# Shared experts of the second layer: fp32 matmuls replaced by three fp32r products of high and low parts

## What is computed

```python
scores = softmax(xt @ gate_w.T); _, idx = top_k(scores + gate_bias, 2)
for e in range(8):
    h = silu(xt @ w1[e].T) * (xt @ w3[e].T)
    y = y + gate_e[:, None] * (h @ w2[e].T)
z = silu(xt @ sw1.T) * (xt @ sw3.T) @ sw2.T        # the shared experts: 512 hidden numbers
return y + z
```

## Time and profile before

| | |
|---|---|
| median of 3 runs | 1104.73 us (1104.25 to 1109.32) |
| the profiled execution | 1107.14 us, of it 1105.3 us from the first to the last instruction |
| granted TensorE clock, mean | 0.894 |
| busy: TensorE, VectorE, GpSimd, ScalarE | 904.4, 696.2, 538.2, 441.5 us |
| gate and up of layer 1's shared experts (L1585) | 128 records, 66.1 us busy |
| their down products (L1632) | 128 records, 28.6 us busy |

### The profile page before, as it was taken

The page is one execution under the profiler, slowest core; times in us unless marked ns, Lnnn a source line. Parts: engine busy times, 40 slices in busy tenths (PEclk is TensorE's granted clock), DMA queues, the critical chain, the costliest instruction groups (busy, mean ns, idle before and its releaser), DMA issues.

```text
span 1105.3 us, 20321 instructions
## 1 busy us (share of the span) xinstructions
PE 904.4 (82%) x5372; PEld 692.5 (63%) x5373; DVE 696.2 (63%) x2004; ACT 441.5 (40%) x1030; POOL 538.2 (49%) x575
## 2 busy tenths in 40 slices
PE   3468888887297999999999904879999996998893
PEld 2357777777144888888888502545656563787672
DVE  6669999996664865555555256765868246443334
ACT  4558888992051444444444302122322313232220
POOL 7246656644004755555552577874700000687641
PEclk9679999995556999999999966969999998899997
DMA  8860000003101777777768738342300011466647
GB/s 248 212 123 3 1 0 0 0 1 107 43 1 51 220 219 202 224 215 220 214 192 138 281 95 278 105 141 80 112 6 20 1 61 23 82 111 127 139 75 243
DMA packets 75225, 127.42 MB, mean 115 GB/s; under 512 B 12481, under 2 KB 52033, under 8 KB 75009
## 3 DMA queue, kind: packets, MB, share of 16 engines
q0 software_dynamic: 21264, 48.02, 19.5%
q1 hardware_dynamic: 32240, 57.47, 17.1%
q10 hardware_dynamic: 21632, 20.85, 5.4%
HBM read 80.62 MB, written 36.77 MB: 106 GB/s over the span
## 4 chain that ended last, share of the span: by engine, by line
PE 60%; DVE 19%; issue 6%; DMA 6%; POOL 3%; ACT 2%; SPq 2%; DVEq 0%; ACTq 0%; POOLq 0%
PE bank L899 18%; PE bank L914 9%; PE bank L1585 5%; PE bank L888 4%; DVE ptl L609 4%; PE bank L801 3%; DMA sw<-in_w 3%; POOL yg L1178 3%; PE bank L1485 3%; DVE nmax L601 2%; PE bank L907 2%; PE bank L419 2%; DVE x L1193 2%; PE bank L1520 2%; PE bank L1632 2%
## 5 line engine op out<-in xcount | busy, mean ns | idle before, releaser
L1163 POOL DMA_INDIRECT xg<-token_rows,gather_idx x198 | 190.7, 963 | 318.3 <-DMA token_rows<-cw 135.6
L899 PE MATMUL bank<-sw,xgt 128*128 x948 | 247.5, 384 | 0.0
L899 PEld LDWEIGHTS bank<-sw,xgt 128*128 128x128 f32 x948 | 167.6, 193 | 15.2
L1178 POOL DMA_INDIRECT yg<-slot_rows,slot_of x128 | 137.0, 1070 | 70.3 <-issue 33.5
L992 ACT ACTIVATE ssil<-bank 128x128 f32<-128x128 f32 x237 | 65.7, 278 | 202.1 <-PE bank L899 202.1
L914 PE MATMUL bank<-sw,sht 128*128 x474 | 145.0, 388 | 0.0
L1084 DVE COPY xgt<-bank 128x256 f32<-128x256 f32 x198 | 83.9, 424 | 85.4 <-PE bank L888 77.3
L1097 DVE COPY sht<-bank 128x128 f32<-128x128 f32 x237 | 69.1, 291 | 106.4 <-PE bank L907 106.1
L537 ACT ACTIVATE prob<-bank,nmax 128x256 f32<-128x256 f32 x256 | 111.7, 511 | 7.5 <-DVE nmax L601 7.5
L419 PE MATMUL bank<-consts,prob 128*128 128x128 f32 x512 | 83.5, 288 | 34.7 <-DVE ptl L609 32.2
L601 DVE TENSOR_REDUCE nmax<-bank 128x2 f32<-128x512 f32 x128 | 87.6, 685 | 16.6 <-PE bank L406 15.7
(11 more groups left out here) (216 smaller groups left out, 1570.5 us busy)
## 6 DMA issues: line engine op xcount, KB each, us to landing
slot_rows<-ysb ACTq DMA_DIRECT2D x79, 256.0 KB, 3.4
sw<-in_w SPq DMA_DIRECT2D x48, 384.0 KB, 3.6
kst<-khl SPq DMA_DIRECT2D x32, 224.0 KB, 5.6
token_sums<-zeros SPq DMA_DIRECT2D x2, 2176.0 KB, 12.1
token_rows<-xn SPq DMA_DIRECT2D x8, 512.0 KB, 3.6
sums<-token_sums SPq DMA_DIRECT2D x8, 512.0 KB, 7.2
xg<-token_rows,gather_idx POOLq DMA_INDIRECT x198, 3.5
x<-in_x SPq DMA_DIRECT2D x4, 512.0 KB, 6.7
```

The source lines that it names most:

```text
L899: mm = pe.matmul(bank[2 + k % 2][:, 0:2 * FF], xgt[:, i % 3, c * P:(c + 1) * P], w[:, :, c, :], start=(c == 0), stop=(c == CH - 1))
L1163: nc.gpsimd.indirect_dma_start(xg[:, (first + i) % XG_RING, 0:ROW[L]], None, rows[L], bass.IndirectOffsetOnAxis(gather_idx[:, i:i + 1], 0) ...
L1178: nc.gpsimd.indirect_dma_start(yg[:, t % Y_TILES, j, :], None, ybuf[L], bass.IndirectOffsetOnAxis(slot_of[:, t, j:j + 1], 0)).then_inc(s_y ...
```

## The change

Both sides of the shared experts' matmuls of layer 1 are split into a high part (the fp32 number copied to the type fp32r) and a low part (the number less its high part, as fp32r), and each fp32 product becomes three fp32r products: high by high, high by low, low by high, summed in PSUM.

- The weights are split once at the start of the stage. They are loaded into two tiles that are used later in the stage (`prob1`, and `hq` as `down_raw`), now ahead of the parameters on SyncE's queue; ScalarE makes `whi` by four copies, VectorE makes `wlo` by four subtractions between its first and its second `y_pair_added`.
- The inputs: after `inputs_copied`, ScalarE makes `xh` (two copies of 512 columns, `inputs_high`), and VectorE makes `xl` (two subtractions, `inputs_low`), placed ahead of `logits_taken`. `shared_gate_up(b, 0)` waits for `xl`.
- The hidden numbers: ScalarE makes `hh` (`hidden_high`, one copy for each of 4 units), and `hl` (`hidden_low`, one subtraction for each) is made by VectorE for batches 0 and 3 and by GpSimd, behind all its gathers, for batches 1 and 2. For batch 3 this happens inside the expert blocks of layer 1. `shared_down` waits for `hl`.

```diff
...
-        wsh1 = sb("wsh1", [P, SH1, WCOLS], F32)
+        whi = sb("whi", [P, SH1, WCOLS], F32R)
+        wlo = sb("wlo", [P, SH1, WCOLS], F32R)
+        xh = sb("xh", [P, CH, SEQ], F32R)
+        xl = sb("xl", [P, CH, SEQ], F32R)
...
+                if L == 1 and 2 <= k < 2 + 2 * SH1 and k % 2 == 0:
+                    hidden_high(act, m, BATCH - 1, (k - 2) // 2)
...
+                if L == 1 and 6 <= k < 6 + 2 * SH1 and k % 2 == 0:
+                    hidden_low(dve, nc.vector, BATCH - 1, (k - 6) // 2)
...
-                if b == 1:
-                    sp.dma_start(wsh1[:, :, :], w1_in[0:SH1].rearrange("u p c -> p u c")).then_inc(m.wload, 16)
...
                 if u == 0:
                     pe.wait_ge(A["p"], 4 * min(b + 2, BATCH))
+                    pe.wait_ge(A["xlo"], CH * (b + 1))
...
-                        mm = pe.matmul(bank[half][:, :], wsh1[:, u, w], xt[:, 0, c, :], start=(c == 0), stop=(c == CH - 1))
+                        for wp, xp in ((whi, xh), (whi, xl), (wlo, xh)):
+                            mm = pe.matmul(bank[half][:, :], wp[:, u, w], xp[:, c, :], start=(n == 0), stop=(n == 5))
+                            n += 1
...
-            pe.wait_ge(m.h, m.n["h"] + SH1 * (b + 1))
+            pe.wait_ge(A["hlo"], SH1 * (b + 1))
...
-                    mm = pe.matmul(bank[6 + j // 2][:, (j % 2) * DIM:(j % 2 + 1) * DIM], hid1[:, u, j * P:(j + 1) * P],
-                                   wsh1[:, u, 2 * CH * FF:WCOLS], start=(u == 0), stop=(u == SH1 - 1))
+                    for hp, wp in ((hh, whi), (hh, wlo), (hl, whi)):
+                        mm = pe.matmul(bank[6 + j // 2][:, (j % 2) * DIM:(j % 2 + 1) * DIM], hp[:, u, j * P:(j + 1) * P],
+                                       wp[:, u, 2 * CH * FF:WCOLS], start=(n == 0), stop=(n == 3 * SH1 - 1))
+                        n += 1
...
+        def hidden_high(act, m, b, u):
+            act.wait_ge(m.h, m.n["h"] + SH1 * b + u + 1)
+            nc.scalar.activation(hh[:, u, :], hid1[:, u, :], ACT.Copy).then_inc(A["hhi"], 1)
+
+        def hidden_low(eng, ops, b, u):
+            eng.wait_ge(A["hhi"], SH1 * b + u + 1)
+            ops.tensor_tensor(hl[:, u, :], hid1[:, u, :], f32(hh[:, u, :]), ALU.subtract).then_inc(A["hlo"], 1)
...
+            def inputs_high(b):
+                if b:
+                    act.wait_ge(m.up, m.n["up"] + SH1 * b)
+                for c in range(CH):
+                    act.wait_ge(m.xh, m.n["xh"] + 2 * b + c + 1)
+                    nc.scalar.activation(xh[:, c, :], xt[:, 0, c, :], ACT.Copy).then_inc(A["xhi"], 1)
...
+            def inputs_low(b):
+                for c in range(CH):
+                    dve.wait_ge(A["xhi"], CH * b + c + 1)
+                    nc.vector.tensor_tensor(xl[:, c, :], xt[:, 0, c, :], f32(xh[:, c, :]), ALU.subtract).then_inc(A["xlo"], 1)
...
             y_pair_added(dve, 0, 0)
+            n = 0
+            for part, source in ((gate_up_cols, prob1), (down_cols, down_raw)):
+                for u in range(0, SH1, 2):
+                    n += 1
+                    dve.wait_ge(A["whi"], n)
+                    nc.vector.tensor_tensor(wlo[:, u:u + 2, part], source[:, u:u + 2, :], f32(whi[:, u:u + 2, part]),
+                                            ALU.subtract).then_inc(A["wlo"], 1)
             y_pair_added(dve, 0, 2)
...
                 encoder(b)
+                if b == 2:
+                    hidden_low(dve, nc.vector, 0, 3)
...
                 if b:
+                    inputs_low(b - 1)
                     logits_taken(b - 1)
...
+                if b == 1:
+                    hidden_low(dve, nc.vector, 0, 0)
                 products(b)
...
         def pool_a1(pool):
             for t in range(TILES):
                 y_gathered(pool, 0, t)
+            for b in (1, 2):
+                for u in range(SH1):
+                    hidden_low(pool, nc.gpsimd, b, u)
...
```

More of the change, by code:

```diff
@@ L134, in gated_xattn_moe_kernel @@
         wsh0 = sb("wsh0", [P, WCOLS], F32)
-        wsh1 = sb("wsh1", [P, SH1, WCOLS], F32)
+        whi = sb("whi", [P, SH1, WCOLS], F32R)
+        wlo = sb("wlo", [P, SH1, WCOLS], F32R)
+        xh = sb("xh", [P, CH, SEQ], F32R)
+        xl = sb("xl", [P, CH, SEQ], F32R)
         hid1 = sb("hid1", [P, SH1, SEQ], F32)
+        hl = sb("hl", [P, SH1, SEQ], F32R)
+        hh = sb("hh", [P, SH1, SEQ], F32R)
         lg1 = sb("lg1", [P, TILES, E1], F32)
@@ L201, in gated_xattn_moe_kernel @@
         hq = sb("hq", [P, CH, SEQ], F32, a1)
+        down_raw = hq[:, :, :].rearrange("p c (a f) -> p (c a) f", f=DIM)
+        gate_up_cols, down_cols = slice(0, 2 * CH * FF), slice(2 * CH * FF, WCOLS)
         prod = sb("prod", [P, CH, SEQ], F32, a1)
@@ L330, in gated_xattn_moe_kernel @@
             "msim", "mx", "mxt", "nmx", "gmx", "ngmx", "eb", "ebr", "hb", "hbc", "w14", "hq", "hqh", "prod", "o", "x",
-            "one", "bg", "bx")}
+            "one", "bg", "bx", "whi", "wlo", "xhi", "xlo", "hhi", "hlo")}
         s_out = sem("out_stored")
@@ L1576, in shared_gate_up @@
                 if v == 0:
-                    pe.wait_ge(m.wload, 16)
+                    pe.wait_ge(A["wlo"], SH1)
                 else:
@@ L1650, in softmax @@
             def softmax(b):
+                if b == 0:
+                    act.wait_ge(A["wlo"], SH1)
                 for j in range(TPB):
@@ L1680, in shared_silu @@
                 nc.scalar.activation(hid1[:, u, :], bank[0][:, :], ACT.Silu).then_inc(m.sil, 1)
+            def inputs_high(b):
[4 more added lines that the diff above has]
+                    nc.scalar.activation(xh[:, c, :], xt[:, 0, c, :], ACT.Copy).then_inc(A["xhi"], 1)
+            act.wait_ge(m.wload, 32)
+            for part, source in ((gate_up_cols, prob1), (down_cols, down_raw)):
+                for u in range(0, SH1, 2):
+                    nc.scalar.activation(whi[:, u:u + 2, part], source[:, u:u + 2, :], ACT.Copy).then_inc(A["whi"], 1)
             for b in range(BATCH):
@@ L1686, in scalar_a1 @@
                     inputs_copied(b - 1)
+                    inputs_high(b - 1)
                     shared_silu(b - 1, 0)
@@ L1692, in scalar_a1 @@
                     for u in range(1, SH1):
+                        hidden_high(act, m, b - 1, u - 1)
                         shared_silu(b - 1, u)
+                    hidden_high(act, m, b - 1, SH1 - 1)
             b = BATCH - 1
             inputs_copied(b)
+            inputs_high(b)
             act.wait_ge(m.rs, 2)
@@ L1849, in vector_a1 @@
                 weights_by_bar(b)
+                if b == 1:
+                    hidden_low(dve, nc.vector, 0, 1)
                 if b:
@@ L1853, in vector_a1 @@
                     y_pair_added(dve, 0, 4 * b + 6)
+                    if b == 1:
+                        hidden_low(dve, nc.vector, 0, 2)
                     stats_of_summed(dve, b + 1)
@@ L1864, in vector_a1 @@
             shared_added(dve, m, b - 1)
+            inputs_low(b)
             logits_taken(b)
@@ L1935, in _ @@
             sp.wait_ge(s_sye, BLOCKS[0])
+            raw = w1_in[0:SH1].rearrange("u p c -> p u c")
+            sp.dma_start(prob1[:, :, :], raw[:, :, 0:2 * CH * FF]).then_inc(moe[1].wload, 16)
+            sp.dma_start(down_raw, raw[:, :, 2 * CH * FF:WCOLS]).then_inc(moe[1].wload, 16)
             parameters_a1(sp)
```

1 line of the change is left out of this document (added).

## The result

The changed kernel took **1124.17 us** (median of 4 runs, 1121.90 to 1126.22) beside 1106.54 us (1104.25 to 1109.32) of the kernel before (4 runs): a ratio of 1.0168, 95% interval 1.0133 to 1.0204. The forecast was 1111, reckoned from the median of 1104.73 of the three runs known then, with a range of 1101 to 1120: the sign was right, the size was not, and the time lies outside the range. The profiled execution took 1126.22 us (span 1124.3, mean clock 0.880) against 1107.14 (1105.3, 0.894).

The account below looks back on a forecast made before the run. TensorE was taken to bound the kernel, VectorE close behind. Turns' shift 0, clock +4.3 and weights' split +2 summed to +6.3 us on the profiled 1107.14; against the median of 1104.73 the forecast was 1111, range 1101 to 1120.

Parts of the forecast that it names:

- TensorE's saving: Shared experts' matmuls: 0.9 us saved per gate and up unit, 1.5 per down product; 20.4 us in all, 18.9 to be won.
- Turn 1: Transposes of turn 2 come 1.7 us earlier; VectorE, making `xn` late, has become the bound there.
- The two waits: Turn 2: TensorE idles 4.4 us before the down product for `hl`, 3.1 behind the logits for `xl`; turn 3 repeats it.
- the clock term: New gaps in turns 2 and 3 bring 2.5 falls to half clock, 1.7 us each: +4.3 us, bounds 0 to 9.
- the forecast gain of 1.9: Batch 3: faster units take back about 1.9 us, so the shift is 0 when the expert blocks begin.
- the split: Stage start: VectorE's four weight subtractions lengthen a GpSimd gather, +2 us, bounds 0 and 3.8; `whi` costs nothing.
- Its literal reading: Port lock held over the back-to-back weight subtractions: split term 3.8 us, sum 1.8 us more; not used in the sum.
- The expert blocks: Layer 1: the four `hh` and `hl` fit between a block's other steps, priced at 0; without cover 4 x 0.65 us.
- (a): Rival: the saving comes through as operands are ready before TensorE asks; about 14 us won, 1091 us; chance 0.14.
- (b): Rival: waits as forecast, but no more clock falls and gathers don't suffer; shift 0, about 1105 us; chance 0.24.
- (c): Rival: half clock through most of turns 2 and 3, or slow fp32r matmuls at 512 columns; 1119 to 1135 us; chance 0.12.

Follow-up runs that it names:

- early_split: Changed kernel with raw weights loaded during layer 0 and split by GpSimd in idle time ahead of its gathers; 1117.82 us, ratio 1.0110.
- reordered: Changed kernel with turns 2 and 3 reordered: down products halved around the scores, input low parts ahead of the shared experts' addition, normalisation later; 1113.68 us, ratio 1.0076.
- filled: Changed kernel with unread fp32r matmuls put into TensorE's waits for `hl` and `xl` in turns 2 and 3; 1116.77 us, ratio 1.0110.
- split_alone: Kernel before plus only the raw weights' loads and their split at the stage's start, results unused, products plain fp32; 1109.81 us, ratio 1.0033.
- loads_alone: Kernel before plus only the raw weights' two loads first on SyncE's queue, no copies or subtractions; 1107.16 us, ratio 1.0021.
- combined_mixed: combined_again with turn 1's four hidden low parts on GpSimd, behind tile 13 and within tiles 14 and 15, not VectorE; 1100.41 us, ratio 0.9959.
- combined_again: Changed kernel with early_split's split and reordered's turns, batch 2's down product left in place, row terms and `xl` products later; repeat run, 1094.12 us, ratio 0.9902.
- combined_pool: combined_again with turn 1's four hidden low parts on GpSimd behind the gathers of tiles 12 to 15, not VectorE; 1104.00 us, ratio 0.9996.

## Why the prediction was wrong, and where it was right

**TensorE's saving** was sized a little high. The down records stand 0.12 us apart at full clock (797.92 to 798.04), 48 of them 5.8 us for a forecast 5.5; a unit of turn 1 at full clock (762.66 to 765.19, 11 records) is 2.75 for 2.6. At these distances a unit saves 0.76 us and a down product 1.2, which makes 16 us of the 18.9, as an estimate.

**Turn 1** came out to the tenth, -1.7, and that is partly luck. The reason given holds: the transposes at 786.20 wait 0.52 us for `xn`, where before there was no wait. But 1.2 of the 1.7 us were won ahead of the first new product, because a half-clock stretch lasted 6.8 us in place of 10.2 at the turn's scores. These scores, before and in the changed kernel:

```profile
722.48 10.06 PE L1485 MATMUL bank<-craw,aenc 128*128 128x512 f32 x16 [1.58 <-issue]
```

```profile
728.42 8.79 PE L1494 MATMUL bank<-craw,aenc 128*128 128x512 f32 x16 [1.58 <-issue]
```

From there on only 0.4 us came, with a fall at 768.90 in the way. In early_split, reordered and filled, which have neither the shorter stretch nor that fall, the turn won 1.1 to 1.4 us.

**The two waits** were placed rightly and sized well: 4.08 us for 4.4; at the second a shift of +2.9 for +3.0, of which 1.74 us were idle and most of the rest was logits at half clock. Turn 3 repeated them with 2.76 and 2.57.

**The step that failed most is the clock term**, "I count 2.5 falls: +4.3 (0 to 9 as bounds)". Both factors were too small. A fall came at each of four places in turns 2 and 3, the step counted three: two began inside the waits for `hl` (789.40 and 854.26), two during the logits between the waits for `xt` and `xl` (809.88 and 874.76). One more came in the third unit of turn 2 (833.78), with no wait of note ahead of it. And each of the four stretches lasted 6.8 us, where I had taken the 3.4 of the earlier trace rows. In batch 3, where the kernel before has two of 3.4, there are two of 6.8, which used up the forecast gain of 1.9. Half-clock work costs 13.2 us from turn 2 on by the table above, and in the same rows of the table the measured column exceeds the forecast by 12.2 (2.3 - 0.1 + 4.3 + 3.5 + 2.2), so the term of 4.3 was 8 to 9 us short. For the two falls in the waits for `hl` filled shows the cause: with the wait unchanged and its gap filled, the product behind it runs at full speed. For the falls ahead of `xl` and at 833.78 the cause stays open.

**The second step that failed is the split**, "I take +2, near the 1.9 of the row" with bounds of 0 and 3.8. It was +6.8 in the changed kernel and +5.5 in split_alone. Most of it is the gather that stood through the subtractions (+5.1, and +3.9 in split_alone). The rest is the late start of the gathers behind the new loads (2.0, and 1.8), for which the forecast had no term. The 2.86 us of the earlier trace rows were no price for such a meeting: the gather had met only the tail of the adds, and in all five kernels looked at (before, loads_alone, early_split, split_alone, changed) the last gather to meet the burst ended 0.8 us behind the burst's end. The bound of 3.8 should have been the value, and the moment of meeting should have been left open above it.

The Trainium skill, SBUF — State Buffer (SBUF: two separate sides), calls the port shared by VectorE and GpSimd an exclusive lock whose loser fully blocks. Its literal reading, set aside in the prediction, agrees with split_alone: 3.9 us more for 3.64 us of subtractions. It also agrees with the other direction in combined_mixed, where VectorE lost 2.7 us to 2.49 us of GpSimd's work. In loads_alone a gather of 1.28 us passed during the adds, so a gather does not always stand for the whole burst.

**The expert blocks** at 0 were right within what one execution shows: they took 141.5 us before and 142.7 after, but also 136.7 in split_alone, where their code is that of the kernel before.

**The rivals.** (a) failed as the changed kernel stands, but what it rests on proved true: with the operands in time most of the saving comes through (1094 in combined_again, where (a) said 1091). (b) had the waits and failed on the clock and the gathers; the full clock behind the 1.70 us wait, which spoke for it, was not there in the changed kernel. (c) named the clock, but as a state of most of two turns; it is in stretches of 3.4 and 6.8 us.

Open: why one fall lasts 3.4 and another 6.8 us (behind the same 4.08 us wait 3.4 in early_split and 6.8 in the changed kernel), and what part of the 0.9 us of turn 0 is the clock, was not tried.

## What to carry to other kernels

A new wait on the busiest engine can cost the slower clock besides the wait: here 4 us of waiting came with a stretch of 6.8 us at half speed, 4.9 of it behind the wait, and the product there lost 2 us more; look in the profile for the longest half-clock stretch, not the nearest. Work that a change splits off for other engines must be placed by who waits for it and by what is queued behind it; with the same products the kernel was 1.7% slower or 1% faster by the places of the split, the low parts and the down product. Where VectorE and GpSimd work from SBUF side by side on a path, put the upper bound of a meeting at the whole burst, in both directions.

## What the runs showed of the hardware

- The clock can fall at a gap whatever the matmuls are: fp32 and fp32r products behind the same 4.08 us wait both began at 0.50 (8.76 and 8.0 us in place of 7.2 and 5.8), and with the gap filled the clock stayed at 1.00 through the wait and the product.
- fp32r matmuls with a new stationary side each time start 0.23 us apart at 512 columns and 0.12 at 256 at full clock, and 0.43 and 0.21 at half.
- One of VectorE's four tensor-scalar steps in combined_mixed took 3.25 us beside two subtractions of GpSimd (2.49 us), the other three 0.41; a 4-element step in combined_pool took 1.85 us instead of 0.16 beside one subtraction:

```profile
777.94 1.85 DVE L751 TENSOR_TENSOR root_step<-root_step,rstd 128x4 f32<-128x4 f32 x1
```
